# Edge attention of a two-layer graph network: weighing and scaling moved from VectorE to ScalarE, transposes moved within the round, three stash lists changed

## The reference

```python
h = max(layernorm(x), 0)
score = sum(h[src] * h[dst])                       # per edge
a = softmax of score over the edges of one dst
agg = segment_sum((h[src] @ W_conv + b_conv) * a, dst)
out = agg + relu(h @ W_res + b_res)
x = x + batchnorm(out)                             # statistics over all nodes
# second layer: per edge gelu(gelu([h[src], h[dst], edge_attr] @ W_m1) @ W_m2),
# summed by dst, then two dense products per node, added to x
```

## Time and profile before

| | |
|---|---|
| median of 3 executions | 1614.78 us (1612.29 to 1616.57) |
| the profiled execution, own time | 1613.91 us |
| its span, first to last instruction | 1612.1 us |
| TensorE matmul busy | 1289.8 us (80%) |
| VectorE busy | 1231.4 us (76%) |
| GpSimd busy | 1108.3 us (69%) |
| ScalarE busy | 942.0 us (58%) |
| mean granted TensorE clock | 0.869 |

### The profile page before, as it was taken

One profiled execution on the slowest core, in us unless ns is written; L12 is line 12 of the kernel. 1 busy time (PEld: TensorE's weight loads), 2 busy tenths in 40 slices (PEclk: granted clock), 3 DMA queues, 4 the chain that ended last, 5 costly groups with the idle time before them and its releaser, 6 DMA issues.

```text
span 1612.1 us, 21905 instructions
## 1 busy us (share of the span) xinstructions
PE 1289.8 (80%) x6227; PEld 786.1 (49%) x6227; DVE 1231.4 (76%) x2432; ACT 942.0 (58%) x1647; POOL 1108.3 (69%) x989
## 2 busy tenths in 40 slices
PE   3566666588778878679989999999849999999982
PEld 2344344377667767544444445444424454454430
DVE  8899997798998998667767677777547777777661
ACT  6599898332332323267777777776526676666651
POOL 7688888777777777777777416767776545455356
PEclk9788888667766766889999999999979999999996
DMA  7577674787864443545556546664645454454410
GB/s 240 182 251 249 221 239 156 249 303 254 296 224 124 140 132 108 202 136 178 187 190 205 174 169 209 212 197 139 208 139 169 131 155 134 144 161 129 124 52 16
DMA packets 141969, 287.34 MB, mean 178 GB/s; under 512 B 33104, under 2 KB 50614, under 8 KB 141852
## 3 DMA queue, kind: packets, MB, share of 16 engines
q1 hardware_dynamic: 109532, 255.32, 47.2%
q0 software_dynamic: 32320, 30.62, 8.3%
HBM read 165.47 MB, written 121.80 MB: 178 GB/s over the span
## 4 chain that ended last, share of the span: by engine, by line
PE 49%; DVE 18%; POOL 12%; issue 9%; ACT 6%; DMA 3%; SPq 2%; DVEq 0%; POOLq 0%; ACTq 0%
PE banks L1512 6%; PE banks L1489 6%; POOL gout L612 5%; POOL x_ring L612 5%; PE banks L1536 4%; PE banks L1418 3%; PE banks L1609 3%; PE banks L1607 3%; PE banks L1616 3%; PE banks L1435 3%; PE banks L1522 3%; DVE sums L844 3%; ACT cT L1239 2%; PE banks L1502 2%; DVE gout L1019 2%
## 5 line engine op out<-in xcount | busy, mean ns | idle before, releaser
L616 POOL DMA_INDIRECT out<-agg,put_last x196 | 198.9, 1015 | 172.8 <-DVE agg L1051 117.8
L612 POOL DMA_INDIRECT agg_ring<-agg_rows,edge_idx x196 | 213.7, 1090 | 131.0 <-DMA edge_agg<-agg_ring 69.5
L612 POOL DMA_INDIRECT x_ring<-in_x,edge_idx x200 | 247.9, 1240 | 73.4 <-issue 63.5
L612 POOL DMA_INDIRECT gout<-in_x,edge_idx x192 | 227.7, 1186 | 58.5 <-issue 57.6
L616 POOL DMA_INDIRECT agg_rows<-agg,put_first x196 | 219.0, 1117 | 59.7 <-issue 57.9
L1374 PE MATMUL banks<-ident,xc 128*128 128x128 f32 (+1 forms) x296 | 58.7, 365 | 103.0 <-DVE xc L772 95.4
L1238 ACT ACTIVATE cT<-banks,packed 96x512 f32<-96x512 f32 (+1 forms) x98 | 66.8, 682 | 112.3 <-PE banks L1512 112.3
L966 DVE TENSOR_TENSOR xc<-banks,xc 128x512 f32<-128x512 f32 (+1 forms) x74 | 51.2, 692 | 98.3 <-PE banks L1536 97.1
L743 DVE TENSOR_REDUCE stat<-sq 128x16 f32<-128x1024 f32 (+1 forms) x98 | 118.7, 1211 | 4.4 <-ACT sq L1224 4.4
L1512 PE MATMUL banks<-hT,packed 64*96 64x512 f32 (+1 forms) x392 | 115.8, 670 | 2.7 <-ACT hT L1231 2.7
L1374 PEld LDWEIGHTS banks<-ident,xc 128*128 128x128 f32 (+1 forms) x296 | 46.8, 188 | 126.5 <-DVE xc L772 96.8
(11 more groups left out here) (195 smaller groups left out, 3427.5 us busy)
## 6 DMA issues: line engine op xcount, KB each, us to landing
xt<-in_x SPq DMA_DIRECT2D x48, 512.0 KB, 6.7
xe<-edge_x SPq DMA_DIRECT2D x96, 256.0 KB, 3.7
agg_rows<-rb SPq DMA_DIRECT2D x48, 512.0 KB
xt<-in_x_t SPq DMA_DIRECT2D x36, 512.0 KB, 5.1
out<-xc SPq DMA_DIRECT2D x36, 512.0 KB, 3.2
r_rows<-rT SPq DMA_DIRECT2D x32, 512.0 KB, 6.6
edge_r<-rr SPq DMA_DIRECT2D x48, 256.0 KB, 4.0
rT<-r_rows SPq DMA_DIRECT2D x24, 512.0 KB, 6.2
```

What stands on the lines that cost most here:

```text
L612: A.indirect_dma_start(to, None, table[:, :], bass.IndirectOffsetOnAxis(ap=idx, axis=0), bounds_check=limit, oob_is_err=False).then_inc(si ...
L616: A.indirect_dma_start(table[:, :], bass.IndirectOffsetOnAxis(ap=idx, axis=0), rows_of, None, bounds_check=limit, oob_is_err=False).then_i ...
```

## The change

- `edge_weight` (VectorE, one operation of 128x256) becomes `weigh_edges` on ScalarE: four operations of 128x64, each with its weight as a scale per partition, in the same round as the exp.
- `edge_finish` is split. VectorE keeps the reciprocal and the product with `first` (`edge_shares`), now placed in the middle of `invert`. The scaling into `agg` becomes `share_agg` on ScalarE, four operations of 128x64 that read PSUM.
- TensorE's `transpose_weighted` stands at the end of the same round, ahead of the statistics, instead of at the head of the next.
- ScalarE's order changes around these.
- SyncE's lists: 9i//10 x groups stashed by round i of stage one (was 6i//7), then `before` + 4(i+1)//3 (was 6(i+1)//5), and for agg min(46, 10(i-12)//3) (was min(40, 3(i-12))).

```diff
-                due = 6 * i // 7
+                due = 9 * i // 10
-                due = min(G, max(before + 6 * (i + 1) // 5, a + 6))
+                due = min(G, max(before + 4 * (i + 1) // 3, a + 6))
-                due = min(40, max(stashed, 3 * (i - STASH)))
+                due = min(46, max(stashed, 10 * (i - STASH) // 3))
...
-            def edge_finish(n):
+            def edge_shares(n):
                 g = group_of(n)
                 p = edges_of(g)
                 dve.wait_ge(E_acc.sem, E_acc.after(n))
+                E_f.done(dve, n - 2)
                 i_ = inv[n % 2][0:p, :]
-                V.reciprocal(i_, acc[:, :, D]).then_inc(E_f.sem, 1)
...
-                V.tensor_tensor(here, acc[:, :, 0:D], per_row(i_), ALU.mult).then_inc(E_f.sem, 1)
+                V.reciprocal(i_, acc_of(n, p)[:, :, D]).then_inc(E_sh.sem, 1)
+                dve.wait_ge(E_sh.sem, E_sh.after(n, 1))
+                V.tensor_tensor(i_, i_, first[0:p, g * EJ:(g + 1) * EJ], ALU.mult).then_inc(E_sh.sem, 1)
...
+            def weigh_edges(n):
+                p = edges_of(group_of(n))
+                w = weighted[n % 2]
+                act.wait_ge(E_exp.sem, E_exp.after(n))
+                for j in range(EJ):
+                    ins = A.activation(w[0:p, j, 0:D], ec[n % 4][0:p, (2 * j + 1) * D:(2 * j + 2) * D], ACT.Copy,
+                                       scale=w[0:p, j, D:D + 1])
+                ins.then_inc(E_w.sem, 1)
+
+            def share_agg(n):
+                g = group_of(n)
+                p = edges_of(g)
+                act.wait_ge(E_sh.sem, E_sh.after(n))
+                for j in range(EJ):
+                    ins = A.activation(agg_of(g, p)[:, j * D:(j + 1) * D], acc_of(n, p)[:, j, 0:D], ACT.Copy,
+                                       scale=inv[n % 2][0:p, j:j + 1])
+                ins.then_inc(E_f.sem, 1)
...
             for i in range(PAIRS + 2):
                 a, b = 2 * i, 2 * i + 1
-                for n in (a, b):
-                    if is_group(n - 4):
-                        square_agg(n - 4)
+                for n in (a - 4, b - 4):
+                    if is_group(n):
+                        share_agg(n)
                 if is_group(a):
                     copy_heT(a)
                     edge_exp(a)
+                if is_group(a - 4):
+                    square_agg(a - 4)
+                if is_group(a):
+                    weigh_edges(a)
                     relu_edges(a)
                 if is_group(b):
                     copy_heT(b)
                     edge_exp(b)
-                for n in (a + 2, b + 2):
-                    square_group(n)
+                if is_group(b - 4):
+                    square_agg(b - 4)
+                if is_group(b):
+                    weigh_edges(b)
+                square_group(a + 2)
                 if is_group(b):
                     relu_edges(b)
+                square_group(b + 2)
...
             for i in range(PAIRS + 2):
                 a, b = 2 * i, 2 * i + 1
-                for n in (a - 2, b - 2):
-                    if is_group(n):
-                        transpose_weighted(n)
                 if is_group(a):
                     transpose_edges(a)
...
                 if is_group(b - 2):
                     conv_product(b - 2)
+                for n in (a, b):
+                    if is_group(n):
+                        transpose_weighted(n)
                 for n in (a - 4, b - 4):
                     if is_group(n):
                         edge_stats(n)
```

More of the change, by code:

```diff
@@ L274, in program @@
         E_st = slots("edge_r_stored", 6)
-        E_f = stage("agg_ready", 3)
+        E_sh = stage("edge_shares_ready", 2)
+        E_f = stage("agg_ready")
         E_ra = stage("agg_times_r")
@@ L377, in agg_of, with acc_of @@
             return agg[0:p, g * EW:(g + 1) * EW]
+        def acc_of(n, p):
+            return bank(n % 2)[0:p, 0:EJ * (D + 1)].rearrange("p (j d) -> p j d", d=D + 1)
         def idx_of(a, g, j, p):
@@ L828, in edge_score @@
                 V.tensor_reduce(score[n % 2][0:p, :], rows(prod[0:p, :]), AX, ALU.add).then_inc(E_sc.sem, 1)
[L830 to L835, removed]
             def edge_scan(n):
@@ L851, in edge_finish @@
                 dve.wait_ge(E_acc.sem, E_acc.after(n))
-                acc = bank(n % 2)[0:p, 0:EJ * (D + 1)].rearrange("p (j d) -> p j d", d=D + 1)
+                E_f.done(dve, n - 2)
                 i_ = inv[n % 2][0:p, :]
-                here = rows(agg_of(g, p))
-                V.reciprocal(i_, acc[:, :, D]).then_inc(E_f.sem, 1)
-                dve.wait_ge(E_f.sem, E_f.after(n, 1))
-                V.tensor_tensor(i_, i_, first[0:p, g * EJ:(g + 1) * EJ], ALU.mult).then_inc(E_f.sem, 1)
-                dve.wait_ge(E_f.sem, E_f.after(n, 2))
-                V.tensor_tensor(here, acc[:, :, 0:D], per_row(i_), ALU.mult).then_inc(E_f.sem, 1)
+                V.reciprocal(i_, acc_of(n, p)[:, :, D]).then_inc(E_sh.sem, 1)
+                dve.wait_ge(E_sh.sem, E_sh.after(n, 1))
+                V.tensor_tensor(i_, i_, first[0:p, g * EJ:(g + 1) * EJ], ALU.mult).then_inc(E_sh.sem, 1)
             def edge_agg_r(n):
@@ L871, in _ @@
                 a, b = 2 * i, 2 * i + 1
-                for n in (a, b):
-                    if is_group(n):
-                        edge_center(n)
-                    if is_group(n - 2):
-                        edge_weight(n - 2)
                 pair = [n for n in (a, b) if is_group(n)]
+                for n in pair:
+                    edge_center(n)
                 for n in pair:
@@ L880, in _, with shares @@
                     sum_squares(estat(1, n, p), esq[n % 2][0:p, :], E_sq, n, E_ss)
+                def shares():
+                    for n in (a - 4, b - 4):
+                        if is_group(n):
+                            edge_shares(n)
                 if pair:
[L882 to L885, removed]
+                    invert(i, P, 2 * R, 2 * R + ER * len(pair), E_inv, E_ss, pair[-1], shares)
+                else:
+                    shares()
                 for n in (a, b):
@@ L1413, in conv_product @@
                 pe.wait_ge(E_scan.sem, E_scan.after(n))
-                E_f.part(pe, n - 2, 3)
+                E_f.done(pe, n - 2)
                 if n < 2:
```

## The result

The changed kernel takes 1622.57 us (median of 8 runs, 1616.48 to 1625.22) against 1612.86 for the kernel before on the same chip (median of 8): ratio 1.0054, 95% interval 1.0039 to 1.0070. The forecast was 1617. The profiled execution has a span of 1621.9, 9.8 more than before.

A forecast was written before the change was run, and what follows sets the result against it. No engine was taken to bound the whole; in attention VectorE was busy 336 of 383 us, and SyncE would then follow the gathers. -5.8 + 8.1 = +2.3 us on 1613.9, the median 0.9 above: 1617 us, range 1596 to 1627 (own range 1609 to 1623).

The forecast's parts named there:

- -5.8 for attention: Edge attention: -0.9 up to round 22, -2.2 for the two rounds left, -2.7 to the statistics' reduction; bounds -13 and +2.
- First list: SyncE's x stashes ahead of attention: 21 instead of 20 before the first edge loads, so attention starts 10.4 us later, at 301.
- the step: ScalarE in attention: 16 more operations at 300 ns, 4.8 us per round on about 4.4, hidden by its idle time.
- A free round: Attention round not held by stashes, paced by VectorE and TensorE: 12.45 to 14.1 us; bounds 12.4 and 15.35.
- Second list: SyncE's x stashes during attention: rounds follow gathers at 15.1 us, round 20's list passes at 609, round 22 starts near 618.3.
- GpSimd: Gathers of x in attention: 11.3 us per group, last issued at 608.2, landed at 610.7, taken as 609.
- rival B: GpSimd's last gather lands 5 us sooner, attention gives -13 and the third list costs +2: 1603 us, chance 0.22.
- Third list: SyncE's agg stashes: held for groups 42 and 45 ahead of edge loads, until 1187 against 1178.9: +8.1 us, bounds 0 to +12.
- A: Rival: SyncE does not hold attention, which gains 31.1 and 2.7 us, with +8.1 behind it: 1589 us, chance 0.13.
- C: Rival: lists cost and compute gives nothing, as TensorE's 1.2 GHz rounds take 16.4 us; attention +2, agg list +9: 1625, chance 0.25.

The follow-up runs named there:

- e5: Changed kernel with all three stash lists as before the change, so the moved work alone: 1592.41 us, ratio 0.9871 to the kernel before.
- e7: Changed kernel with 19 stashes ahead of attention, masks first each round, and a slacker agg list: 1088.5 us behind attention, on a chip with stalls.
- e12: Changed kernel with the first x list of before, the second one stash fewer, and a slack agg list: 1081.5 us behind attention, on a chip with stalls.
- e2: Changed kernel with all three stash lists as before the change, the code of e5, on a chip with stalls: ratio 1.0074 to the kernel before.

## Why the prediction was right, and where its terms were off

The forecast's sum was -5.8 for attention and +8.1 for the agg list. Measured: +1.0 and +8.8. So the forecast was a difference of +2.3 us, too small to be told from none; the measured one is +9.8 on the profiled executions, and its interval leaves no room for none. The mechanism is the predicted one, and the term that was mis-sized is attention's, by 6.8 us. That the time of 1622.57 lies just inside the narrower range (1609 to 1623) is partly luck, since the kernel before came out at 1612.86 and not 1614.8.

*First list: right.* The stash of group 20 goes at 293.28 (forecast 293.0), the first subtraction at 301.68 (301).

*ScalarE: there is room for the work, but it isn't wholly hidden, and the step was too long.* The `Copy` operations take 336 and 324 ns each (medians; forecast for one alone 335), and ScalarE's busy time grows by 82.3 us for 392 of them, 0.21 us each where I took 0.30. The slope of 0.69 ns per column behind the 335 compares an operation that reads SBUF (417 ns) with one that reads PSUM (594); the squares from SBUF, 256 columns in 417 and 512 in 619 ns (kernel before), give 0.79. By groups of lines in attention:

```profile
L1167 ACT ACTIVATE weighted<-ec_wide,weighted 128x64 f32<-128x64 f32 (+1 forms) x196 | 51.6, 337 | 0.1
...
L1176 ACT ACTIVATE agg<-banks,inv 128x64 f32<-128x64 f32 (+1 forms) x196 | 43.1, 329 | 53.8 <-DVE inv L853 53.8
```

Worked out from the figures of the Trainium skill ("ScalarE: Activation LUTs", section "What ACT_TABLE_LOAD costs"), the estimate was 332 ns alone and 240 in a row. The trace agrees with both for the weighings: four in a row last 1.05 us, so (1.05 - 0.336) / 3 = 238 ns a step. Eight scalings from PSUM last 1.75 us, 204 ns a step, less than the estimate.

*VectorE: the range right, at its upper end.* A free round was to take 12.45 to 14.1 us. In e5 the short rounds take 12.7 to 12.9, others up to 16.3, and the mean is 13.97, against 14.97 before (with the short first round in both). So a round gains 1.0 us of the 1.75 taken off VectorE. A wait came up that I had not named and that the kernel before does not have: VectorE for ScalarE's squares (changed kernel, 300 to 674):

```profile
DVE stat L747 <- ACT esq_wide L1153: 37.4, 38, 2.4
```

It is 35.4 us in e5 too, so it costs the moved work and not the lists. Of a round's two squares the first now stands behind a square of agg and the weighings on ScalarE, the second behind `relu_edges` too, which waits for TensorE: 20.9 and 14.5 us of e5's 35.4. This is the part of the moved work that ScalarE's idle time did not hide, where the prediction charged nothing. An order of ScalarE's line without it wasn't tried.

One reading of the clock was coarse: its two levels do not coincide with rounds. In the kernel before it is 1.00 from 430 to 443 and 0.50 from 445 to 460, so the low stretch begins inside the short round and ends in the long one. That it begins behind the 2.62 us without work stands.

*Second list: the mechanism right, one size right and one wrong.* The list holds SyncE, the last gather is where it was forecast, VectorE waits for a mask behind the last stash, and from round 12 on a round takes 15.2 us on average (forecast 15.1). What I had not seen is that this begins only in round 12 (the first twelve take 14.0) and that it comes mainly as one hold in rounds 12 and 13, as said above. Then everything in the last stretch came later than the sum had it: round 22 at 622.06, not 618.3 (+3.8: the list passed at 611.3 and not 609, where the prediction's own 610.7 was lowered for gathers that did not come sooner; the mask issued at 612.6 was used at 617.85, 5.2 us later and not 3.6); the two rounds behind it 29.15, not 28.5 (+0.6); the rest to the reduction 23.4, not 21 (+2.4). These three are the 6.8 us between -5.8 and +1.0. In that rest VectorE stands for TensorE's statistics:

```profile
667.50 0.42 DVE L861 TENSOR_TENSOR ragg<-agg,rr 128x256 f32<-128x256 f32 x1 [3.12 <-PE banks L1471]
```

e5 has 20.8 us there. The granted clock was 1.00 in e5 and 0.85 here, with TensorE busy for 17.6 and 20.7 us, and these 3.1 us cover the 2.6 between the two stretches. The last stash is 40 us past by then, so this part reads as the clock's and not as a wait for a gather; no run tested it.

*GpSimd: right.* Its last gather did not come sooner (608.15 against 608.23) though VectorE has 36.8 us less to do; rival B falls with that, and its +2 for the third list with the measured +8.8.

*Third list: right.* SyncE is held for group 42 until 1187.4 (forecast 1187, before 1178.9), and the rest is 8.8 us longer (forecast 8.1).

*The rivals.* A said SyncE doesn't hold attention. Its time, 1589, is near e5's 1592, but that is chance: A's sum has attention 33.8 us shorter and the new agg list at +8.1, and e5, with the old one, has 26.9 and 0. C had attention (+2) and the total (1625) nearer to the measured +1.0 and 1622.6 than the forecast, but with the wrong cause: e5 shows that the compute gives 26.9 us. The lists take 28 us in attention and 9 behind it, the moved work gives 27: the forecast's +2.3 hid how large its two sides are, since I set the gain of the compute only against rounds already paced by gathers.

## What to carry to other kernels

A queue that takes its list in order should ask for a transfer when a consumer is near, not when a producer could be: every early request is a wait in front of whatever else that queue serves. How early is harmless was not found: the slacker agg lists (e7, e12) can't be told from the old one. Before an edit that frees an engine, write down who paces each stretch once it is free, and cost each schedule change against that faster pace; here the same lists that looked like small moves took more than all of a 1.3% gain. Changes that come together are to be run apart: neither sign nor size of the parts can be seen in their sum.

## What the runs showed that was not expected

On chips 4, 5 and 7 every kernel here took 2052 to 2129 us. Two thirds of the extra time stand in attention. e2 and e5 are the same code: attention starts at 290.6 and 290.5, lasts 702.3 us against 356.2, and the rest behind it 1107.2 against 938.7, so 346 us of the 515 are in attention and 169 behind it. The windows of e2 (columns as in the earlier trace rows): one before attention, the worst stretch, and one behind it.

```profile
0.00:290.00 290.00, 174.65 (x586) 104.28 (x586) 257.69 (x326) 228.54 (x485) 227.81 (x177) 0.82 0.69 220
...
700.00:900.00 200.00, 30.77 (x111) 25.34 (x111) 25.23 (x58) 13.58 (x44) 153.70 (x153) 0.53 0.12 37
900.00:1500.00 600.00, 474.61 (x2539) 269.36 (x2539) 371.95 (x716) 356.24 (x576) 200.01 (x187) 0.88 0.44 147
```

TensorE, VectorE and ScalarE are busy for 13 to 31 of 200 us there, the DMA engines for 12%, while GpSimd goes on with a scatter each 1.28 us. Stage one is untouched. Behind attention there are shorter waits of this kind: up to 22 us of ScalarE in e2. No run tells what the engines wait for.
